# A Fourier-layer kernel: variance from a moment matrix, inverse y product in small tiles, TensorE's sweep as a loop

## The reference, cut to what matters

```python
v = jnp.transpose(h @ p_w + p_b, (0, 3, 1, 2))
for i in range(4):
    x1 = _fourier_layer(v, W1, W2)                       # rfft2, mix 24x12 modes, irfft2
    x2 = jnp.einsum('bcxy,cd->bdxy', v, w_w[i]) + w_b[i][None, :, None, None]
    v = x1 + x2
    mean = jnp.mean(v, axis=(0, 2, 3), keepdims=True)
    var = jnp.var(v, axis=(0, 2, 3), keepdims=True)
    v = (v - mean) * jax.lax.rsqrt(var + BN_EPS)
    v = v * bn_g[i][None, :, None, None] + bn_b[i][None, :, None, None]
    if i < 3:
        v = jax.nn.relu(v)
```

## Time and profile before

| what | value |
|---|---|
| median of 3 runs | 3295.86 us |
| profiled execution, its span, its mean granted PE clock | 3287.43 us, 3285.6 us, 0.891 |
| PE busy (matmul) | 2691.4 us, 82% |
| DVE busy | 2128.4 us, 65% |
| ACT busy | 1400.1 us, 43% |
| POOL busy | 638.5 us, 19% |
| L838 evictions | 384 instructions, 446.3 us |
| L845 squares | 384 instructions, 388.3 us |
| L963 channels | 6144 matmul passes, 243.1 us |
| DMA, mean over the span | 165 GB/s |

### The profile page before, as it was taken

One profiled execution on the slowest core, in us unless ns is written; L12 is line 12 of the kernel. 1 busy time (PEld: TensorE's weight loads), 2 busy tenths in 40 slices (PEclk: granted clock), 3 DMA queues, 4 the chain that ended last, 5 costly groups with the idle time before them and its releaser, 6 DMA issues. The chain is left out here.

```text
span 3285.6 us, 109526 instructions
## 1 busy us (share of the span) xinstructions
PE 2691.4 (82%) x47620; PEld 1506.3 (46%) x47620; DVE 2128.4 (65%) x3099; ACT 1400.1 (43%) x2298; POOL 638.5 (19%) x806
## 2 busy tenths in 40 slices
PE   3489999997999999789999987670647885499999
PEld 1245555553555555345555553220236664144444
DVE  4567777776677877667777775005446776477766
ACT  2545555544455555445555554001101111177776
POOL 3002333110133321103343110000025552000000
PEclk9779899888999999989999998795867775799999
DMA  5166666652888878458888763794222220288886
GB/s 169 18 142 147 137 145 145 144 127 97 273 258 251 265 246 251 152 158 257 258 262 255 247 197 134 310 407 68 61 65 66 67 58 17 55 142 142 142 143 112
DMA packets 243993, 541.29 MB, mean 165 GB/s; under 512 B 77856, under 2 KB 124704, under 8 KB 229952
## 3 DMA queue, kind: packets, MB, share of 16 engines
q1 hardware_dynamic: 234448, 528.03, 59.0%
q10 hardware_dynamic: 9136, 7.12, 1.0%
HBM read 320.28 MB, written 214.78 MB: 163 GB/s over the span
## 5 line engine op out<-in xcount | busy, mean ns | idle before, releaser
L838 ACT ACTIVATE p_v<-p_ps,k_scale_bias 128x1024 f32<-128x1024 f32 x384 | 446.3, 1201 | 635.5 <-PE p_ps L947 635.5
L707 DVE STREAM_TRANSPOSE p_t<-p_ps 128x1024 f32<-128x1024 f32 x192 | 363.7, 1967 | 304.4 <-PE p_ps L700 303.9
L822 POOL COPY k_xm<-p_sp 64x288 f32<-64x288 f32 x384 | 268.9, 700 | 1453.6 <-DVE p_sp L301 1436.9
L947 PEld LDWEIGHTS p_ps<-k_idfty,p_t 64*128 64x128 f32 x6144 | 402.7, 206 | 183.6 <-issue 183.5
L845 ACT ACTIVATE p_ps<-p_ps 128x1024 f32<-128x1024 f32 x384 | 388.3, 1011 | 165.3 <-PE p_ps L963 165.1
L947 PE MATMUL p_ps<-k_idfty,p_t 64*128 64x128 f32 x6144 | 445.4, 299 | 15.4 <-issue 15.3
L291 DVE STREAM_TRANSPOSE p_vt<-p_v 128x1024 f32<-128x1024 f32 x384 | 447.8, 1206 | 0.0
L2039 ACT ACTIVATE x_ht<-x_ph,w_b 128x384 f32<-128x384 f32 x576 | 303.2, 578 | 131.6 <-PE x_ph L2091 131.6
L2068 DVE TENSOR_TENSOR x_ht<-x_ht,x_mask 128x384 f32<-128x384 f32 x512 | 261.7, 555 | 138.8 <-ACT x_ht L2039 89.1
L938 PE MATMUL p_ps<-p_v,k_wbd 32*32 32x512 f32 x4096 | 298.4, 609 | 19.0 <-DVE p_t L707 10.3
L963 PE MATMUL p_ps<-p_v,k_wbd 32*32 32x512 f32 x6144 | 243.1, 605 | 10.4 <-DVE p_sp L301 0.9
(11 more groups left out here) (299 smaller groups left out, 3099.3 us busy)
## 6 DMA issues: line engine op xcount, KB each, us to landing
field<-p_v SPq DMA_DIRECT2D x768, 256.0 KB, 4.6
p_v<-field SPq DMA_DIRECT2D x64, 2048.0 KB
x_mask<-expert_weights SPq DMA_DIRECT2D x32, 1536.0 KB, 14.8
l_v<-field SPq DMA_DIRECT2D x16, 2048.0 KB, 26.3
k_xm<-field SPq DMA_DIRECT2D x12, 2048.0 KB, 24.8
k_mixw<-in_L_tok_fw_dram SPq DMA_DIRECT2D x16, 1152.0 KB, 11.4
at_cf<-state_coefficients SPq DMA_DIRECT2D x32, 384.0 KB
k_mixw<-field SPq DMA_DIRECT2D x4, 2048.0 KB, 24.1
```

Source lines behind the costliest of these rows:

```text
L707: return nc.vector.transpose(st[:, q].rearrange("p x c -> p c x"), ps[:, 2 * q:2 * q + 2, :].rearrange("p j (m c) -> p c j m", c=C))
L822: nc.gpsimd.tensor_copy(view[64 * k:64 * k + 64, :, j, :, G * i:G * i + G], sp[64 * j:64 * j + 64, :, :, 16 * k:16 * k + M1].rearrange("p ...
L838: nc.scalar.activation(field[:, 2 * q:2 * q + 2, CH * half:CH * half + CH], ps[:, e, 2 * q:2 * q + 2, :], ACT.Relu, bias=bias, scale=scale ...
L947: ins = nc.tensor.matmul(ps[:, e, 2 * q + h, col:col + 128], lines, K["idfty"][rows, :], start=False, stop=True, skip_group_check=True)
```

## The change

Three things change in `layer_phase`.

First, the next layer's variance comes from a moment matrix. `channels` and `squares` go. `gram_product` multiplies each of the 128 blocks of 128x32 turned pixels with itself, into a 128x32 piece of PSUM, and DVE adds that to `gacc` once a group (`gram_sum`). In the next phase PE multiplies `gacc` with `wall` (the weights, four more DMAs in `dense_weights`), DVE multiplies by the weights again (`gw`), and one more matmul against `one` gives the sum that `zs` gave.

Second, the inverse products use smaller tiles. `inverse_y` has 64 matmuls of 32x64 weights against 64 columns for each half, and `inverse_x` 32 matmuls of 64x32 weights against 192 columns for a group where there were 16 of 64x64. `st` is laid out so that the inverse turn writes pairs of neighbouring fp32 elements; before, each element that it wrote lay 128 bytes from the last.

Third, order and buffers. PE's work on one group is a turn of a hardware loop, `pe.Fori(2, n - 1)`, 29 turns; groups 0, 1 and 31 stay written out. Column half 0 is in PSUM set 0 and half 1 in set 1, and the forward products of the group before and the spectrum of the group after take the two sets in turn. There is one input buffer, loaded in two halves of 1 MB, whose rows are 2 KB pieces (before, one load with rows of 16 KB); a load waits for `um_done` of the same half of the group before. In layer 0 the grid is loaded once for the layer. Two further buffers take the results, so ACT waits for the stores of two groups back. The other engines stay unrolled.

```diff
...
+        dve.wait_ge(s.gw_done, 1)
+        ve.tensor_tensor(K["gw"][:, :], zb[0:C, 1, 1, 0:P], K["wall"][0:C, :], ALU.mult).then_inc(s.gw_ready, 1)
...
+        pe.wait_ge(s.wall_in, 64)
+        nc.tensor.matmul(zb[0:C, 1, 1, 0:P], K["gacc"][:, :], K["wall"][:, :], start=True, stop=True).then_inc(s.gw_done, 1)
...
+        nc.tensor.matmul(ps[:, 0:1], K["gw"][:, :], K["one"][:, :], start=True, stop=False)
...
+    return nc.vector.transpose(st[:, s].rearrange("p h c x -> p c h x"),
+                               ps[:, 2 * s:2 * s + 2, :].rearrange("p j (m c) -> p c j m", c=C))
...
+def inverse_y(nc, K, ps, st, half):
+    for d in range(2):
+        for b in range(4):
+            for a1 in range(2):
+                for g in range(G):
+                    rows, col = slice(C * g, C * g + C), 256 * d + S * b
+                    lines = st[rows, half, 8 * d + 2 * b:8 * d + 2 * b + 2, :, a1].rearrange("p x c -> p (x c)")
+                    ins = nc.tensor.matmul(ps[64 * a1:64 * a1 + 64, g, col:col + S], lines, K["idfty"][rows, :],
+                                           start=False, stop=True, skip_group_check=True)
+    return ins
...
+def gram_product(nc, ps, vt):
+    for k in range(P):
+        block = vt[:, k // 32, C * (k % 32):C * (k % 32) + C]
+        ins = nc.tensor.matmul(ps[C * (k % 4):C * (k % 4) + C, :], block, block, start=(k < 4), stop=(k >= P - 4))
+    return ins
...
+            def load(i, half):
+                at_least(eng, s.um_done, 2 * i - 1 + half if i else 0)
...
-                store(i, 0)
-                if 3 <= i + 2 < n:
-                    load(i + 2)
-                store(i, 1)
-            for b in range(3):
-                eng.wait_ge(u_out[b], 128 * len(range(b, n, 3)))
+                for half in range(2):
+                    if i + 1 < n:
+                        load(i + 1, half)
+                    store(i, half)
...
-                field = v[:, i % 3].rearrange("p (g m) -> p g m", g=G)
+                field = v[:, 1 + i % 2].rearrange("p (g m) -> p g m", g=G)
+                if i >= 2:
+                    act.wait_ge(u_out[2 * (i % 2) + half], 64 * (i // 2))
+                    act.wait_ge(s.vt_ready, 4 * (i - 2) + 2 * half + 2)
+                act.wait_ge(s.um_done, 2 * i + half + 1)
...
-            def squares(i, e, half):
-                for q in range(2):
-                    act.wait_ge(s.zq_done, 4 * i + 2 * half + q + 1)
-                    at = 4 * i + 2 * half + q
-                    nc.scalar.activation(ps[:, e, 2 * q:2 * q + 2, :], ps[:, e, 2 * q:2 * q + 2, :], ACT.Square,
-                                         accum_out=K["zs"][:, at:at + 1]).then_inc(s.sq_done, 1)
...
-                    elif i == 0:
-                        pe.wait_ge(s.uo_ready, g // 2 + 1)
-                    else:
-                        pe.wait_ge(s.sq_done, 4 * (i - 1) + g // 2 + 1)
...
-                for q in range(2):
-                    for d in range(2):
-                        for b1 in range(2):
-                            for h in range(2):
-                                x = 16 * b1 + 4 * (2 * half + d)
-                                rows, col = slice(64 * h, 64 * h + 64), 256 * d + 128 * b1
-                                lines = st[rows, q, x:x + 4, :].rearrange("p a c -> p (a c)")
-                                ins = nc.tensor.matmul(ps[:, e, 2 * q + h, col:col + 128], lines, K["idfty"][rows, :],
-                                                       start=False, stop=True, skip_group_check=True)
...
-                for a in range(4):
-                    if half == 1:
-                        pe.wait_ge(s.uo_ready, 4 * i + 2 + a // 2 + 1)
-                    elif i + 1 < n:
-                        pe.wait_ge(s.uo_ready, 4 * (i + 1) + a // 2 + 1)
-                    else:
-                        pe.wait_ge(s.sq_done, 4 * (i - 1) + 2 + a // 2 + 1)
-                    if a == 0:
-                        pe.nop(nofuse=True)
-                    for g in range(G):
-                        rows, col = slice(C * a, C * a + C), 1024 * g + CH * half
-                        ins = nc.tensor.matmul(ps[C * g:C * g + C, e, a, :], K["wbd"][rows, 1, rows], v[rows, i % 3, col:col + CH],
-                                               start=True, stop=True)
...
+                inverse_y(nc, K, ps[:, e], st, half).then_inc(s.um_done, 1)
...
+                if more:
+                    pe.wait_ge(s.uo_ready, 4 * i + 6)
...
+            def moments(i, more):
+                if more:
+                    pe.wait_ge(s.uo_ready, 4 * i + 7)
+                else:
+                    pe.wait_ge(s.gm_ready, i)
+                pe.nop(nofuse=True)
+                gram_product(nc, ps[:, 1, 0, 0:C], vt).then_inc(s.gm_done, 1)
...
-            for i in range(n):
-                e = i % 2
+            pe.wait_ge(s.t_ready, 1)
+            for i in range(2):
+                pixels(i, 0)
+                pixels(i, 1)
                 if i >= 1:
-                    at_least(pe, s.sp_ready, i - 1)
-                    channels(i - 1, 1 - e, 1)
-                pixels(i, e, 1)
-                if i + 1 < n:
-                    spectrum(i + 1, 1 - e)
-                if i >= 1:
-                    pe.wait_ge(s.uo_ready, 4 * i + 4)
-                    y_product(i - 1, e)
-                if i + 1 < n:
-                    pixels(i + 1, 1 - e, 0)
-                if i >= 1:
-                    x_product(i - 1, e)
-                channels(i, 1 - e, 0)
-            pe.wait_ge(s.sp_ready, n - 1)
-            channels(n - 1, 1, 1)
-            pe.wait_ge(s.sq_done, 4 * (n - 1) + 2)
-            y_product(n - 1, 0)
-            x_product(n - 1, 0)
+                    forward(i - 1, True)
+                spectrum(i + 1)
+            with pe.Fori(2, n - 1) as i:
+                pixels(i, 0)
+                pixels(i, 1)
+                forward(i - 1, True)
+                spectrum(i + 1)
+            pixels(n - 1, 0)
+            pixels(n - 1, 1)
+            forward(n - 2, True)
+            forward(n - 1, False)
...
```

More of the change, by code:

```diff
@@ L499, in channel_weights, with dense_weights @@
         eng.dma_start(K["wbd"][rows, slot, rows], par["w_w"][layer]).then_inc(done, 16)
+def dense_weights(eng, s, K, par, layer):
+    for q in range(4):
+        src = par["w_w"][layer].rearrange("c (o d) -> c o d", o=1).broadcast_to([C, G, C])
+        eng.dma_start(K["wall"][C * q:C * q + C, :].rearrange("p (o d) -> p o d", o=G), src).then_inc(s.wall_in, 16)
 def mix_scalar(nc, act, s, K, M, first, raw):
@@ L601, in mix_tensor @@
         at_least(pe, s.zt_done, 2 * (n - 1))
+        if n == 1 and not first:
+            pe.wait_ge(s.gw_ready, 1)
         if n == 2:
@@ L625, in mix_tensor, with norm_vector @@
         ins.then_inc(s.mix_done, 1)
[L628 removed]
+def norm_vector(nc, dve, s, K, B, first, scale_bias, w, t, st, ones, ps):
     ve = nc.vector
@@ L689, in norm_tensor, with inverse_x @@
         nc.tensor.matmul(ps[:, 3:6], ones[:, :], K["gram"][:, 0:3], start=True, stop=True)
-    nc.tensor.matmul(ps[:, 0:1], K["groupsum"][:, :], t[:, 0:1], start=True, stop=True)
+    else:
+        pe.wait_ge(s.gw_ready, 1)
+        nc.tensor.matmul(ps[:, 0:1], K["gw"][:, :], K["one"][:, :], start=True, stop=False)
+    nc.tensor.matmul(ps[:, 0:1], K["groupsum"][:, :], t[:, 0:1], start=first, stop=True)
     nc.tensor.matmul(ps[:, 1:3], K["groupsum"][0:C, :], st[:, 6:8], start=True, stop=True).then_inc(s.pe_step, 1)
-def inverse_x(nc, K, ps, yt, q):
+def inverse_x(nc, K, ps, yt, s):
@@ L696, in inverse_x @@
     for t in range(2):
-        for h in range(2):
-            for j in range(2):
+        for j in range(2):
+            for g in range(G):
                 rows = slice(64 * j, 64 * j + 64)
-                ins = nc.tensor.matmul(ps[64 * h:64 * h + 64, 2 * q + j, 192 * t:192 * t + 192], K["idftx"][rows, t, :],
-                                       yt[rows, :, 2 * q + h, :], start=True, stop=True)
-    return ins
-def turn_inverse(nc, st, ps, q):
-    return nc.vector.transpose(st[:, q].rearrange("p x c -> p c x"), ps[:, 2 * q:2 * q + 2, :].rearrange("p j (m c) -> p c j m", c=C))
+                ins = nc.tensor.matmul(ps[C * g:C * g + C, 2 * s + j, 192 * t:192 * t + 192], K["idftx"][rows, t, C * s:C * s + C],
+                                       yt[rows, :, g, :], start=True, stop=True)
@@ L738, in layer_phase @@
         n_1 = ctx.enter_context(nc.sbuf_tensor(f"n_1{tag}", [P, P if first else 1], F32))
-        u_in, u_out = [s.u_in0, s.u_in1, s.u_in2], [s.u_out0, s.u_out1, s.u_out2]
-        loads = 8 if first else 1
+        u_in, u_out = [s.u_in0, s.u_in1], [s.u_out0, s.u_out1, s.u_out2, s.u_in2]
+        loads, before = (8, 4) if first else (1, 0)
         view = spectra(K)
@@ L921, in _, with pixels @@
             depth, weights = (4, K["pwbd"][:, :]) if first else (C, K["wbd"][:, 0, :])
-            def pixels(i, e, half):
-                b = i % 3
```

(38 more changed lines are left out.)

171 lines of the change are left out of this document (87 added, 84 removed).

## The result

The changed kernel takes 3318.8 us (median of 7 runs, 3307.9 to 3324.8), against 3295.0 for the kernel before on the same chips: ratio 1.0067, 95% interval 1.0049 to 1.0086. It is 0.7% slower, where the forecast was no change. Its profiled span is 31.4 us longer than before, 7 us of it in the experts' products, which the change doesn't touch (from the first to the last start of L2091, now L2121, it is 431.2 us in the trace of before and 438.0 after; the traces of the experiments have 433.0 to 439.4). The medians are 23.8 us apart, because the profiled execution of before was 8 us faster than its median.

What follows compares the result with a forecast made beforehand. PE was taken to set the pace. Layers 1 and 2 gain 33 us, layer 0 loses 28, the variance costs 3: -2. So 3287.4 - 2 + 8.4 = 3294 us, range 3150 to 3480.

Steps and rivals of the forecast that it cites:

- Layer 0, the step that failed: Layer 0's sweep: 17.0 us a turn, 587 us in all against 559 before, a loss of 28.
- The paragraph on loads: SP's load issues: two of 1 MB where there was one, 0.34 us each, beside everything else.
- the clock term: Layer 0: PE's granted clock drops in each turn as before, adding 1.9 us to 15.1.
- A turn in layers 1 and 2: Kept loop turns: PE's work 15.1 us and the chain through DVE 15.0, so 15.1 against 16.67 before.
- The price of a pass: New short matmuls on PE: 16.7 ns each, giving moments 3.9 us and inverse y 1.8 a half.
- the prediction's own sign of being wrong: Moments on PE: the prediction is wrong if 256 passes take under 3 or over 5 us.
- the first rival: Passes start faster and fetches are shorter: moments near 2.4 us, 126 us less, about 3168; chance 0.29.
- The bounds for DMA: DMA time a group: 14.2 to 17.3 us over 16 engines; low end taken, high end +123 us.
- Inverse turn 1.2 us: DVE's inverse turn, writing pairs: 1.2 us where it took 1.9; bounds 1.16 and 1.9.
- The loop is kept: PE's loop of 6.1 blocks stays in the instruction buffer, so 28 of 29 turns fetch nothing.
- The chance of 0.08 against it: Third rival: the loop isn't kept and each turn fetches 6.1 blocks, 25.6 us; about 4120 us, chance 0.08.
- Written-out code at 4.2 us a block: Instruction fetch for groups 0, 1, 31, forward products and first turn: 23.6 blocks, 99 us for each layer.

Runs made afterwards that it cites:

- e1: Layer 0's image half loaded in two DMAs instead of eight, against the changed kernel; 3182.5 us, 0.9672 of the kernel before.
- e7: Layers 1 and 2 store only half of the columns, the same number of DMAs, on top of e1; one run of 3113.1 us.
- e9: Inverse turn writes single elements 128 bytes apart again, on top of e5; one run of 3204.5 us.
- e8: The changed kernel with PE's 29 loop turns written out in the same order; one run of 4240.9 us.
- e10: 64 of the 128 moment matmuls of a group made twice, on top of e5; a single run of 5087.6 us.
- e4: Group 2 also written out, so PE's loop starts at group 3, against the changed kernel; one run of 3361.4 us.
- e5: PE's loop covers groups 1 to 31, with one unused inverse x product, on top of e1; 3117.7 us, 0.9467 of the kernel before.

## Why the prediction was wrong

The prediction said no change, 3294 us; the result, 3318.8, lies in its range, but it is clear of no change, on the slower side. Its mechanism, a shorter turn in a kept loop paid for by written-out code and by layer 0, is what the runs show. One term had the wrong cause and the wrong size, and an error on the other side hid part of it. That the total came within 25 us of the forecast is in part luck.

- **Layer 0, the step that failed.** I took its turn at 15.1 + 1.9 = 17.0 us, the 1.9 for a granted clock that I carried over from the trace of before. The turn is 18.1 to 18.3 and its cause is SP's queue: 28 x 1.2 = 34 us more. The paragraph on loads counted two issues a turn "beside everything else". In layer 0 the diff's own inner loop issues eight for a half, sixteen for a group, in front of and between the stores. The trace of before had a price for such an issue:

```profile
L759 SPq DMA_DIRECT2D p_v<-in_x_dram x128: 625/637/1147, 125.7 to 693.7; - x128
```

Sixteen at 0.64 us are 10.2 us of SP's queue, before any store. With four loads a turn in place of sixteen, the turn is 13.4 (e1), so the queue costs 4.7 us in a turn and the clock term should have been 0. No rival had SP's queue in it.

- **A turn in layers 1 and 2: 15.1 forecast, 14.4 and 14.6 measured**, 28 x 0.7 + 28 x 0.5 = 34 us less. The price of a pass was the mis-sized term: 16.7 ns taken, 10.4 measured for the moments and 12.7 for the inverse y product. With 2.67 us for the moments, which meets the prediction's own sign of being wrong (under 3), and 1.62 for each inverse y product, PE's sum is 13.5, and e1 has 13.4 in layer 0. The price is close to the one of the first rival; the time is not, because DMA traffic holds the turn at 14.4 (e7). The bounds for DMA, 14.2 to 17.3 us a turn, were both too high as the engines' own time: a packet took 0.916 x 300 x 16 / 45989 = 0.096 us, not 0.111, and the engines were busy for 13.2 us of a turn. That 14.4 lies near the low bound is luck.
- **Inverse turn 1.2 us**: right (L726, 225.4 us for 192, against the earlier trace rows); e9 shows that it was needed.
- **The loop is kept**: right (no packet on q8 from 1000 to 1300 us, and e8). The chance of 0.08 against it was not idle: e10 shows the loop within one block of losing everything.
- **Written-out code at 4.2 us a block**: nearly right. e4 gives 4.2 to 4.8, e5 4.4, e8 4.3 to 4.5, and a sweep of the changed kernel fetches 23 blocks where 23.6 were counted. Outside the 28 kept turns a sweep took 526 - 28 x 14.4 = 123 us in layer 1, where 111 were forecast; the head alone, from 872 to 960 us, fetched 15 blocks in 88 us, with the start of the pipeline in it. Layer 2 is much the same: some 11 us more in each.
- **The third sweep before** was read 4.4 us too long (552 for 547.5), and the other two 1 us together, so 5 of the forecast's gain was not there to be had.
- **The variance on the path**: +3 forecast. The stretches between the sweeps, 66.9 and 70.3 us before, are 66.5 and 70.8 now, so nothing of it shows there.
- **What is outside the sweeps**: 11 us more in the profiled traces, 7 of it in the experts' products. The change doesn't explain it, and the traces of the experiments vary by 6 us in those products alone; it was not followed further.

Together: the sweeps were forecast at 587 + 534 + 534 us and took 20 more (34 in layer 0, -34 for the shorter turns, 21 in their ends, and -1). 3294 + 20 + 5 for the sweeps of before, + 8 outside (11 where 3 were forecast), - 8.4, because the profiled execution of the changed kernel is itself the median run, gives 3318.6; 3318.8 was measured.
